# A graph network's edge scores: four-pair waits before the scatters, a full score ring, hot rows turned before the sums, mix steps over pairs 6 to 74

## Chip, cores and metric

One Trainium2 chip, one core. The time is the device time of one execution in microseconds (us): the median of three runs.

## The reference, cut to what matters

Two layers of a graph network over 625 nodes and 20,000 edges, 256 channels. The change lies wholly in layer 0, in the stage that computes one score per edge and head, and beside which the "mix" block of the layer is computed:

```python
# layer 0, graph attention (xn: layernorm of x; 4 heads of 64)
xl = (xn @ W_l).reshape(625, 4, 64); xr = (xn @ W_r).reshape(625, 4, 64)
e = leaky_relu(xl[src] + xr[dst], 0.2)
score = einsum('ehd,hd->eh', e, att)            # one score per edge and head
alpha = softmax of score over the edges of one dst
agg = segment_sum(alpha * xl[src], dst)
# layer 0, mix block on the same xn (8 heads of 32, rank 4)
h = layernorm(xn); xm = h @ Wx + bx
q, k, v = softmax(xm @ Wq), softmax over nodes(xm @ Wk), xm @ Wv
fx = (q @ (k.T @ v)) @ Wo + bo + xn
mix = gelu(layernorm(fx) @ W1 + b1) @ W2 + b2 + fx
x = x + gnn + mix        # then two-expert feed-forward, and layer 1
```

## The kernel before, in words

The edges are first sorted into buckets by (tile of dst, tile of src), 25 buckets, in 184 columns of 125 edges each (`SORTED`). Two columns are a pair, so there are 92 pairs (`PAIRS`). For each column the kernel has two one-hot matrices (the node of dst, the node of src) and works so:

- VectorE, `make_hots` (L1248): builds the one-hots of a pair, two pairs ahead.
- TensorE, `turn_hots` (L621 to L623): turns both one-hots of a column and multiplies them (the counts) into bank 4 or 5. It waits for the one-hots and for `counted`, the earlier `add_counts` on that bank.
- ScalarE, `copy_hots` (L1997): copies the turned hots from the bank to `hot`.
- TensorE, `sum_rows` (L643): eight matmuls a pair, four for each column, that gather and add the rows xl[src] + xr[dst] of 125 edges from the split tables `x_hi` and `x_lo`. The address of the tile comes from registers that `load_rows` loads.
- ScalarE, `read_rows` (L2006, L2007): absolute value of the sums into `weighed` (`tc`), and signals `z_read`.
- VectorE, `weigh` (L1273): times `att`; `add_counts` (L1267): adds a column's counts to `cnt`; `score` (L1281): the sum over a head, to `sc_ring`, signals `scored`.
- GpSimd, `scatter` (L2243): two indirect DMAs a pair, one for each column, into two tables in HBM (`pair_scores`). A scatter into a table waits for the landing of the last one into the same table (`scattered0`, `scattered1`), and the first of a pair waits for `scored`, too.

Each engine runs its instructions in the order in which they are written. The loops over the pairs are

```python
# TensorE                          # VectorE                      # ScalarE
sum_rows(i)                        make_hots(i + 2)               copy_hots(2i + 2)
turn_hots(2i + 2)                  add_counts(2i + 2)             copy_hots(2i + 3)
turn_hots(2i + 3)                  weigh(i)                       read_rows(i)
mix(i)                             add_counts(2i + 3)             mix(i)
load_rows(i + 1)                   score(i); load_counts; mix(i)
```

`mix(i)` is the piece of the mix block whose key in `MIX` is i: a part on TensorE, on ScalarE and on VectorE, in most pairs none. Hidden tiles `m1` take eight pairs in a row, output tiles `m2` five. When all scatters have landed, SyncE loads the two score tables back (`arena<-pair_scores`), and the attention of layer 0 begins; ScalarE takes the logarithm of the counts in between. Apart from these logarithms nothing of the kernel is written beside the end of the scatters.

Of the kernel before, what the change touches and what calls it, by code (L numbers as in the profile page):

```python
# [30 lines left out]
N, D, E = 625, 256, 20000  # L31
P, T = 125, 5
K2 = D // 128
CHUNKS = [(0, 375, (0, 1, 2)), (375, 250, (3, 4))]
H = 4
# [18 lines left out]
PAIRS = SORTED // 2  # L54
# [5 lines left out]
CHOSEN = 3  # L60
MARKS = SORTED + 1
HOTS = 3
SCORED = 16
MIX_BANKS = 3
ROW = D + H
SUM_BANKS = (6, 7, 3)


MIX = {"ln1": 6, "mixh": 8, "turned": 10, "xm": 11, "qkv_in": 12, "softened": 14, "turned_kq": 15, "kv": 17, "qkv": 18,
       "attn": 20, "ln2": 22, "h2": 23, "h2T": 25, "m1": 26, "m2": 35, "added": 40}  # L70


SORTING = {"member": 1, "sums": 3, "block_counts": 4, "begun": 6, "columns": 7, "ident16": 8, "owners_read": 11,
# [58 lines left out]
def after(eng, sem, value):  # L132

    if not (isinstance(value, int) and value <= 0):
        eng.wait_ge(sem, value)
# [35 lines left out]
def build(nc, x_in, src_in, dst_in, base_in, order_in, vec0_in, vec1_in, fb_in, w0_in, w1_in, w2_in, mixw_in, exp0_in,  # L171
          exp0o_in, exp1_in, exp1o_in, exp1r_in, rope_in, out):
    ctx = ExitStack()
    with ctx:
        sems = {}

        def sem(name):
            if name not in sems:
                sems[name] = ctx.enter_context(nc.semaphore(name))
            return sems[name]  # L180

        def sb(name, shape, dt=F32):
            return ctx.enter_context(nc.sbuf_tensor(name, shape, dt))
# [6 lines left out]
        pair_scores = [nc.dram_tensor(f"pair_scores{i}", [N * NC + P, H], F32).ap() for i in range(2)]  # L190
# [62 lines left out]
        at_rows, at_counts = sb("at_rows", [1, SORTED, 2], I32), sb("at_counts", [1, SORTED], I32)  # L253
        spare_cell = sb("spare_cell", [P, 1])
        by_head = sb("by_head", [P, T, 2, H])
        sc_ring = sb("sc_ring", [P, SCORED, 2, H])
        cnt = sb("cnt", [P, T, N])
        mask_words = sb("mask_words", [128, (T * N + 1) // 2])
        nmask = mask_words[0:P, :].bitcast(BF16)[:, 0:T * N].rearrange("p (t n) -> p t n", t=T)
# [8 lines left out]
        hi_rows, lo_rows = (f[0:P, :, :, :].rearrange("p t w d -> p (t w d)") for f in (x_hi, x_lo))  # L268
        at = 2 * T * 2 * ROW + HOTS * 2 * 2 * P
        slot_parts = arena[0:P, at:at + BUCKETS * EC].rearrange("p (b j) -> p b j", b=BUCKETS)  # L270
        w_by_att = arena[:, at:at + K2 * 2 * D].rearrange("p (k n) -> p k n", k=K2)
        at += BUCKETS * EC
        assert at <= ARENA - FF // 128 * (D + N)
        at = ARENA - FF // 128 * N
# [9 lines left out]
        at = 6 * EC  # L284
# [35 lines left out]
        at = ARENA - FF // 128 * (D + N)  # L320
# [10 lines left out]
        at = 5 * H * NC  # L331
# [3 lines left out]
        at = 0  # L335
# [7 lines left out]
        at = 2 * IN1  # L343
# [78 lines left out]
        def read_out(eng, *key):  # L422

            last = {}
            for name, (b, _, n) in ticket.items():
                if name[:len(key)] == key:
                    last[b] = max(last.get(b, 0), n)
            assert last, key
            for b, n in last.items():
                eng.wait_ge(free[b], n)  # L430
# [33 lines left out]
        def _(pe):  # L464
# [18 lines left out]
            def to_fm(name, src):  # L483

                for k in range(K2):
                    for c, (off, w, tiles) in enumerate(CHUNKS):
                        bank, done = group((name, k, c))
                        for t in tiles:
                            mm = pe.transpose(bank[:, t * P - off:t * P - off + P],
                                              src[:, t, k * 128:(k + 1) * 128], ident[0:P, 0:P])  # L490
                        mm.then_inc(done, 1)
# [20 lines left out]
            def linear_fm(name, f, weights, m_tiles, ks=K2):  # L512

                for m in range(m_tiles):
                    for c, (off, w, _) in enumerate(CHUNKS):
                        bank, done = group((name, m, c))
                        for k in range(ks):
                            mm = pe.matmul(bank[:, 0:w], W(weights, k)[:, m * 128:(m + 1) * 128],
                                           f[:, k, off:off + w], start=(k == 0), stop=(k == ks - 1))
                        mm.then_inc(done, 1)  # L520
# [94 lines left out]
            def turn_hots(c):  # L615

                pe.wait_ge(sem("onehot"), c // 2 + 1)
                after(pe, sem("counted"), c - 1)
                bank = banks[4 + c % 2]
                to_d, to_s = (onehot[:, c // 2 % TAKEN, :, c % 2 * 2 + w] for w in range(2))  # L620
                pe.matmul(bank[0:P, 0:P], to_d, ident16[:, :], start=True, stop=True)  # L621
                pe.matmul(bank[0:P, P:2 * P], to_s, ident16[:, :], start=True, stop=True)  # L622
                pe.matmul(bank[0:P, 2 * P:3 * P], to_d, to_s, start=True, stop=True).then_inc(sem("turned_hots"), 1)  # L623
# [3 lines left out]
            def load_rows(i):  # L627

                _, rows_at[i] = nc.values_load_multi_w_load_instructions(
                    at_rows[0:1, 2 * i:2 * i + 2, :].rearrange("p c w -> p (c w)"), engines=[mybir.EngineType.PE],  # L630
                    min_val=0, max_val=(2 * T - 1) * ROW,
                    skip_runtime_bounds_check_because="each is a sum of tile steps over the buckets begun, a tile's offset")

            def sum_rows(i):

                rows = rows_at.pop(i)
                for c in range(2):
                    pe.wait_ge(sem("hot"), 2 * i + c + 1)
                    after(pe, sem("z_read"), 2 * i + c - 2)
                    n = 0  # L640
                    for w in range(2):
                        for part in (hi_rows, lo_rows):
                            mm = pe.matmul(banks[SUM_BANKS[(2 * i + c) % 3]][0:P, 0:ROW], hot[0:P, i % HOTS, c, w, :],  # L643
                                           part[:, bass.ds(rows[2 * c + w], ROW)], start=(n == 0), stop=(n == 3))
                            n += 1
                    mm.then_inc(sem("z_made"), 1)
# [18 lines left out]
            def mix(i):  # L665

                if i == MIX["turned"]:
                    pe.wait_ge(sem("w0_in"), 16)
                    pe.wait_ge(sem("mixh"), 1)
                    to_fm("mixhT", ta)  # L670
                elif i == MIX["xm"]:
                    read_out(pe, "mixhT")
                    linear_fm("xm", fb_, "wx", K2)
                elif i == MIX["qkv_in"]:
                    read_out(pe, "xm")
# [7 lines left out]
                    for c, (off, w, _) in enumerate(CHUNKS):  # L683
# [4 lines left out]
                        mm.then_inc(done, 1)  # L688
                elif i == MIX["turned_kq"]:
                    pe.wait_ge(sem("ksoft"), 1)  # L690
# [5 lines left out]
                    for c, (off, w, tiles) in enumerate(CHUNKS):  # L696
# [3 lines left out]
                        mm.then_inc(done, 1)  # L700
                elif i == MIX["kv"]:
                    read_out(pe, "kN")
# [4 lines left out]
                    mm.then_inc(done, 1)  # L707
                elif i == MIX["qkv"]:
                    read_out(pe, "kv")
# [41 lines left out]
            turn_hots(0)  # L751
            turn_hots(1)
            for i in range(PAIRS):
                sum_rows(i)
                for c in (2 * i + 2, 2 * i + 3):
                    if c < SORTED:
                        turn_hots(c)
                mix(i)
                if i + 1 < PAIRS:
                    load_rows(i + 1)  # L760
# [261 lines left out]
        def _(dve):  # L1022
            own = Chain(dve, sem("dve_own"))
            v = nc.vector
# [39 lines left out]
            def from_fm(name, dst):  # L1064

                for c, (off, w, _) in enumerate(CHUNKS):
                    bank, freed = got(dve, (name, 1, c))
                    v.tensor_copy(dst[:, 1, off:off + w], bank[:, 0:w]).then_inc(freed, 1)
# [185 lines left out]
            def load_counts(i):  # L1254

                _, count_at[i] = nc.values_load_multi_w_load_instructions(
                    at_counts[0:1, 2 * i:2 * i + 2], engines=[mybir.EngineType.DVE], min_val=0, max_val=T * N - P,
                    skip_runtime_bounds_check_because="each is a sum of steps over the buckets begun, a bucket's offset")
# [16 lines left out]

            def score(i):

                for w in range(2):
                    after(dve, sem(f"scattered{w}"), 16 * (i - SCORED + 1))
                own.fence()  # L1280
                v.tensor_reduce(sc_ring[:, i % SCORED, :, :].rearrange("p c h -> p (c h)"),  # L1281
                                weighed[:, i % 2, :, :, :].rearrange("p c h d -> p (c h) d"), AX.X, ALU.add)\
                    .then_inc(sem("scored"), 1)

# [893 lines left out]
        def _(pool):  # L2178
            p = nc.gpsimd
# [57 lines left out]

            def scatter(c):
                which, i = c % 2, c // 2
                if which == 0:  # L2240
                    pool.wait_ge(sem("scored"), i + 1)
                after(pool, sem(f"scattered{which}"), 16 * i)
                p.indirect_dma_start(  # L2243
                    out=pair_scores[which], in_=sc_ring[:, i % SCORED, which, :], in_offset=None,
                    out_offset=bass.IndirectOffsetOnAxis(ap=pair_cells[:, c:c + 1], axis=0))\
                    .then_inc(sem(f"scattered{which}"), 16)

# [8 lines left out]
            for c in range(SORTED):  # L2256
                scatter(c)
# [231 lines left out]
```

## Time and profile before

| | |
|---|---|
| median of three runs | 1112.62 us (1112.42 to 1114.56) |
| the profiled execution | 1119.57 us, span 1117.8 us |
| TensorE matmul, VectorE, ScalarE, GpSimd busy | 862.5, 766.6, 352.7, 375.2 us |
| `scatter`, L2243 | 184 indirect DMAs, 226.6 us busy, 144.5 us idle before them |
| `sum_rows`, L643 from `x_hi` and from `x_lo` | 368 and 368 matmuls, 119.9 and 102.8 us |
| `weigh` L1273, `score` L1281 | 92 and 92, 64.0 and 63.8 us |

Spans are counted from the first instruction, and the execution's own time lies 1.8 us above its span. The busy time of an engine says little by itself here: most engines work in short pieces that wait for each other, and what matters is which piece is last. The granted clock of TensorE (PEclk) is 1.00 at 2.4 GHz and 0.50 at 1.2 GHz.

### The profile page before, as it was taken

The page shows a single profiled execution, that of the slowest core. Times are in us where ns is not written, and L with a number is a line of the kernel's source. Part 1 is how long each engine was busy: PE and PEld are TensorE (multiplying, and loading weights), DVE is VectorE, ACT ScalarE, POOL GpSimd, SP SyncE. Part 2 cuts the span into 40 slices and gives each one's busy share as a digit, 9 for nine tenths or more (in the row PEclk, how much of TensorE's full clock was granted, in tenths as well). Part 3 has the DMA queues.
Part 4 walks back from the last instruction along what each step waited for, and adds up shares of the span by engine and source line. Part 5 has one row for each costly group of instructions (what it writes and reads, how often), then busy time and mean ns, then how long its engine had stood idle before and what let it go on. Part 6 is the DMA issues. An engine that isn't in the chain of part 4 may idle for free.

```text
span 1117.8 us, 18660 instructions
## 1 busy us (share of the span) xinstructions
PE 862.5 (77%) x5483; PEld 736.2 (66%) x5483; DVE 766.6 (69%) x1980; ACT 352.7 (32%) x1096; POOL 375.2 (34%) x321
## 2 busy tenths in 40 slices
PE   4889679699888881017639999895896787699996
PEld 3578567588766660017538999783586476689895
DVE  7778777855777771028977888577788755766635
ACT  0277434273455553015401111101362062112120
POOL 3287646455677666500002222150000000211104
PEclk9988888699899996558858999996898798699999
DMA  8830000000000000089028999970000000688893
GB/s 282 256 119 1 3 2 3 2 3 2 3 3 4 4 2 3 2 195 229 25 65 282 313 321 318 349 231 23 1 1 1 0 2 14 242 300 296 302 328 95
DMA packets 38282, 129.39 MB, mean 116 GB/s; under 512 B 12885, under 2 KB 20929, under 8 KB 29913
## 3 DMA queue, kind: packets, MB, share of 16 engines
q1 hardware_dynamic: 21742, 112.64, 30.8%
q0 software_dynamic: 10464, 8.67, 4.5%
q10 hardware_dynamic: 5992, 7.04, 1.8%
q8 instruction: 43, 0.70, 0.3%
q14 instruction: 41, 0.34, 0.1%
HBM read 108.83 MB, written 19.26 MB: 115 GB/s over the span
## 4 chain that ended last, share of the span: by engine, by line
PE 57%; DVE 18%; DMA 11%; issue 7%; POOL 4%; ACT 2%; DVEq 0%; POOLq 0%; SPq 0%; ACTq 0%
PE bank L854 12%; PE bank L643 9%; PE bank L865 6%; DMA arena<-pair_scores 4%; PE bank L582 4%; PE bank L787 3%; DMA pair_scores<-sc_ring,pair_cells 2%; PE bank L621 2%; PE bank L623 2%; POOL arena L2277 2%; POOL pair_scores L2243 2%; DMA arena<-slot_y,sloti 2%; PE bank L953 2%; PE bank L622 2%; PE bank L653 2%
## 5 line engine op out<-in xcount | busy, mean ns | idle before, releaser
L2243 POOL DMA_INDIRECT pair_scores<-sc_ring,pair_cells x184 | 226.6, 1232 | 144.5 <-issue 70.8
L2267 POOL DMA_INDIRECT arena<-row_tab,ids x42 | 57.5, 1369 | 501.6 <-DVE ids L1660 494.2
L854 PE MATMUL bank<-arena 128*128 128x128 f32 x1480 | 180.6, 280 | 2.6 <-DMA arena<-in_exp 2.6
L854 PEld LDWEIGHTS bank<-arena 128*128 128x128 f32 x1480 | 174.7, 196 | 4.8 <-DMA arena<-in_exp 4.0
L643 PE MATMUL bank<-x_hi,hot 125*125 x368 | 119.9, 346 | 17.4 <-ACT tc L2007 9.9
L1997 ACT ACTIVATE hot<-bank 125x250 fp32r<-125x250 f32 x184 | 68.8, 379 | 163.8 <-PE bank L623 163.5
L776 PE MATMUL bank<-ident,arena 125*125 125x125 f32 x260 | 44.9, 306 | 85.3 <-ACT arena L2054 84.1
L1273 DVE TENSOR_TENSOR tc<-tc,vec 125x512 f32<-125x512 f32 x92 | 64.0, 696 | 56.8 <-ACT tc L2007 56.8
L643 PE MATMUL bank<-x_lo,hot 125*125 x368 | 102.8, 299 | 0.0
L643 PEld LDWEIGHTS bank<-x_hi,hot 125*125 125x125 f32 x368 | 73.1, 199 | 44.4 <-issue 43.7
L865 PE MATMUL bank<-arena 128*128 128x256 f32 (+1 forms) x404 | 99.1, 389 | 2.9 <-issue 2.9
L776 PEld LDWEIGHTS bank<-ident,arena 125*125 125x125 f32 x260 | 40.0, 214 | 90.1 <-issue 77.9
L865 PEld LDWEIGHTS bank<-arena 128*128 128x128 f32 (+1 forms) x404 | 73.1, 192 | 17.0 <-issue 9.2
L2054 ACT ACTIVATE arena<-arena,rneg 125x625 f32<-125x625 f32 (+4 forms) x60 | 44.9, 748 | 115.2 <-DVE rneg L1474 78.0
L643 PEld LDWEIGHTS bank<-x_lo,hot 125*125 125x125 f32 x368 | 74.3, 202 | 0.6
L2125 ACT ACTIVATE arena<-bank 128x512 f32<-128x512 f32 (+2 forms) x76 | 34.4, 453 | 125.1 <-PE bank L854 124.9
L621 PE MATMUL bank<-ident,mask_words 125*125 125x125 bf16 x184 | 48.6, 264 | 27.5 <-DVE cnt L1267 19.7
L1267 DVE TENSOR_TENSOR cnt<-cnt,bank 125x125 f32 x184 | 51.4, 279 | 22.4 <-ACT hot L1997 21.5
L2006 ACT ACTIVATE tc<-bank 125x256 f32<-125x256 f32 x184 | 66.5, 393 | 0.3 <-PE bank L643 0.3
L1281 DVE TENSOR_REDUCE sc_ring<-tc 125x8 f32<-125x520 f32 x92 | 63.8, 694 | 0.4 <-issue 0.3
L2235 POOL TENSOR_SCALAR fmaps<-iota_c,tab 125x185 bf16<-125x185 f16 x40 | 49.2, 1247 | 43.3 <-DVEq L1153 33.9
L1673 DVE TENSOR_TENSOR arena<-bank,arena 128x512 f32<-128x512 f32 (+2 forms) x76 | 37.2, 508 | 37.2 <-ACT arena L2125 37.1
(397 smaller groups left out, 1747.0 us busy)
## 6 DMA issues: line engine op xcount, KB each, us to landing
arena<-in_exp SPq DMA_DIRECT2D x25, 1024.0 KB, 7.1
arena<-in_exp SPq DMA_DIRECT2D x17, 1386.0 KB, 6.3
arena<-in_exp0o SPq DMA_DIRECT2D x25, 512.0 KB, 7.2
pair_scores<-cnt SPq DMA_DIRECT2D x10, 1093.8 KB
arena<-in_exp1o SPq DMA_DIRECT2D x17, 640.0 KB
arena<-pair_scores SPq DMA_DIRECT2D x7, 1093.8 KB
slot_y<-arena ACTq DMA_DIRECT2D x34, 128.0 KB, 6.4
fmaps<-pair_scores SPq DMA_DIRECT2D x3, 1093.8 KB
```

What stands on the lines that cost most here:

```text
L621: pe.matmul(bank[0:P, 0:P], to_d, ident16[:, :], start=True, stop=True)
L643: mm = pe.matmul(banks[SUM_BANKS[(2 * i + c) % 3]][0:P, 0:ROW], hot[0:P, i % HOTS, c, w, :], part[:, bass.ds(rows[2 * c + w], ROW)], start ...
L776: mm = pe.transpose(bank[0:P, t * P - off:t * P - off + P], prob[:, i % 3, t * P:(t + 1) * P], ident[0:P, 0:P])
L854: mm = pe.matmul(banks[1 + 2 * q + buf][0:rows, i * SLOTS:(i + 1) * SLOTS], w_in(s, q, k, m, rows), xsT[:, s, k, :], start=(k == 0), stop= ...
L865: mm = pe.matmul(banks[5 + s][:, 0:D], hid[0:rows, s, m, :], w_out(s, m), start=(m == 0), stop=(m == len(flat) - 1))
L1267: v.tensor_tensor(to, to, banks[4 + c % 2][0:P, 2 * P:3 * P], ALU.add).then_inc(sem("counted"), 1)
L1273: own.note(v.tensor_tensor(rows, rows, Vt(0, "att").rearrange("p (h d) -> p h d", h=H).unsqueeze(1) .to_broadcast([P, 2, H, HD]), ALU.mult))
L1281: v.tensor_reduce(sc_ring[:, i % SCORED, :, :].rearrange("p c h -> p (c h)"), weighed[:, i % 2, :, :, :].rearrange("p c h d -> p (c h) d") ...
L1997: a.activation(hot[0:P, c // 2 % HOTS, c % 2, :, :].rearrange("p w n -> p (w n)"), banks[4 + c % 2][0:P, 0:2 * P], ACT.Copy).then_inc(sem( ...
L2006: a.activation(rows[:, c, :, 0:HD], bank[0:P, 0:D].rearrange("p (h d) -> p h d", h=H), ACT.Abs, scale=0.4)
L2243: p.indirect_dma_start(out=pair_scores[which], in_=sc_ring[:, i % SCORED, which, :], in_offset=None, out_offset=bass.IndirectOffsetOnAxis( ...
L2267: p.indirect_dma_start(out=xs[:, q, :], out_offset=None, in_=tab, in_offset=bass.IndirectOffsetOnAxis(ap=ids[:, q, :], axis=0))\
```

## The change

Four edits. The scatters of the first four pairs wait for `scored` pair by pair as before; from pair 4 on only every fourth pair waits, and then for all four pairs. `sc_ring` has 92 places in place of 16, lies in a part of `arena` that the sorting has left, and `score` waits for no scatter. On TensorE `turn_hots` of the next pair stands ahead of `sum_rows` of this one. The steps of the mix block lie farther apart, and end at pair 74 in place of 40.

```diff
-SCORED = 16
+SCORED = PAIRS
+AHEAD = 4
-MIX = {"ln1": 6, "mixh": 8, "turned": 10, "xm": 11, "qkv_in": 12, "softened": 14, "turned_kq": 15, "kv": 17, "qkv": 18,
-       "attn": 20, "ln2": 22, "h2": 23, "h2T": 25, "m1": 26, "m2": 35, "added": 40}
+MIX = {"ln1": 6, "mixh": 9, "turned": 12, "xm": 15, "qkv_in": 18, "softened": 21, "turned_kq": 24, "kv": 27, "qkv": 30,
+       "attn": 33, "ln2": 37, "h2": 41, "h2T": 45, "m1": 50, "m2": 66, "added": 74}
...
-        sc_ring = sb("sc_ring", [P, SCORED, 2, H])
+        sc_ring = arena[0:P, at + K2 * 2 * D:at + K2 * 2 * D + SCORED * 2 * H].rearrange("p (s c h) -> p s c h", s=SCORED, c=2)
...
             for i in range(PAIRS):
-                sum_rows(i)
                 for c in (2 * i + 2, 2 * i + 3):
                     if c < SORTED:
                         turn_hots(c)
+                sum_rows(i)
                 mix(i)
...
             def score(i):
-                for w in range(2):
-                    after(dve, sem(f"scattered{w}"), 16 * (i - SCORED + 1))
                 own.fence()
-                v.tensor_reduce(sc_ring[:, i % SCORED, :, :].rearrange("p c h -> p (c h)"),
+                v.tensor_reduce(sc_ring[:, i, :, :].rearrange("p c h -> p (c h)"),
...
             def scatter(c):
                 which, i = c % 2, c // 2
-                if which == 0:
-                    pool.wait_ge(sem("scored"), i + 1)
+                if which == 0 and (i < AHEAD or i % AHEAD == 0):
+                    pool.wait_ge(sem("scored"), i + 1 if i < AHEAD else min(i + AHEAD, PAIRS))
                 after(pool, sem(f"scattered{which}"), 16 * i)
                 p.indirect_dma_start(
-                    out=pair_scores[which], in_=sc_ring[:, i % SCORED, which, :], in_offset=None,
+                    out=pair_scores[which], in_=sc_ring[:, i, which, :], in_offset=None,
```

## Rows read from the trace of the kernel before

**Rows 1.** The chain that ended last, in time: start us, length us, what.
```profile
281.61 2.61 DMA pair_scores<-sc_ring,pair_cells
...
452.05 3.19 DMA pair_scores<-sc_ring,pair_cells
...
474.72 4.05 DMA pair_scores<-sc_ring,pair_cells
480.05 12.99 DMA arena<-pair_scores
```

**Rows 2.** `score`: durations in ns, first and last start; busy | idle before it.
```profile
L1281 DVE TENSOR_REDUCE sc_ring<-tc x92: 681/695/696, 111.8 to 424.2; 125x8 f32<-125x520 f32 x92
...
L1281 DVE TENSOR_REDUCE sc_ring<-tc 125x8 f32<-125x520 f32 x92 | 63.8, 694 | 0.4 <-issue 0.3
```

**Rows 3.** GpSimd in order of time: start, length, and the idle time before.
```profile
310.53 1.19 POOL L2243 DMA_INDIRECT pair_scores<-sc_ring,pair_cells  x1 [0.78 <-issue]
312.03 1.19 POOL L2243 DMA_INDIRECT pair_scores<-sc_ring,pair_cells  x1 [0.30 <-issue]
313.92 1.19 POOL L2243 DMA_INDIRECT pair_scores<-sc_ring,pair_cells  x1 [0.70 <-DVE sc_ring L1281]
```

**Rows 4.** One undisturbed pair, all engines in order of time, clock 1.00.
```profile
326.36 0.28 DVE L1267 TENSOR_TENSOR cnt<-cnt,bank 125x125 f32 x1
...
326.78 0.30 PE L621 MATMUL bank<-ident,mask_words 125*125 125x125 bf16 x1
...
327.03 0.32 PE L623 MATMUL bank<-mask_words 125*125 125x125 bf16 x1
...
327.39 0.38 ACT L1997 ACTIVATE hot<-bank 125x250 fp32r<-125x250 f32 x1 [0.31 <-PE bank L623]
327.39 0.38 PE L643 MATMUL bank<-x_hi,hot 125*125 x1
...
327.98 0.41 ACT L2006 ACTIVATE tc<-bank 125x256 f32<-125x256 f32 x1
328.24 0.21 ACT L2007 ACTIVATE tc<-bank 125x4 f32<-125x4 f32 x1
...
328.35 0.38 PE L643 MATMUL bank<-x_hi,hot 125*125 x1 [0.21 <-ACT tc L2007]
...
328.49 0.69 DVE L1273 TENSOR_TENSOR tc<-tc,vec 125x512 f32<-125x512 f32 x1 [0.69 <-ACT tc L2007]
...
328.81 0.28 PE L643 MATMUL bank<-x_lo,hot 125*125 x1
...
328.93 0.22 PE L621 MATMUL bank<-ident,mask_words 125*125 125x125 bf16 x1
...
329.10 0.28 DVE L1267 TENSOR_TENSOR cnt<-cnt,bank 125x125 f32 x1
```

**Rows 5.** Busy us (and instructions) of each engine by stretch, PEclk, DMA.
```profile
305.60:422.00 116.40, 101.05 (x593) 79.03 (x593) 86.86 (x212) 61.86 (x258) 79.71 (x65) 1.00 0.08 3
128.10:131.50 3.40, 2.38 (x14) 1.65 (x13) 3.30 (x15) 1.45 (x6) 2.37 (x3) 1.00 0.07 2
...
285.10:288.50 3.40, 2.51 (x14) 1.87 (x14) 3.37 (x7) 1.38 (x6) 2.98 (x2) 1.00 0.04 1
288.50:295.30 6.80, 6.36 (x32) 5.92 (x32) 4.77 (x12) 3.68 (x16) 4.81 (x5) 0.50 0.08 3
537.70:554.70 17.00, 10.90 (x94) 10.30 (x93) 16.13 (x45) 7.58 (x21) 0.00 (x0) 1.00 0.01 2
223.70:251.00 27.30, 27.30 (x159) 22.77 (x158) 15.41 (x36) 19.37 (x62) 15.71 (x14) 1.00 0.07 3
```

**Rows 6.** One `sum_rows` at clock 0.50, from the order of time.
```profile
291.65 0.58 PE L643 MATMUL bank<-x_hi,hot 125*125 x1 [0.20 <-ACT hot L1997]
...
292.68 0.42 PE L643 MATMUL bank<-x_hi,hot 125*125 x1
...
293.32 0.42 PE L643 MATMUL bank<-x_lo,hot 125*125 x1
```

## The prediction

> **What bounds the kernel now.** I read the chain of waits first, then the lines of `score` and `scatter`, then one pair instruction by instruction, then the clock by stretch.
>
> The chain shows where the stage ends. The last scatter is issued at 474.72 and lands 4.05 us later, at 478.77; the tables are loaded back from 480.05 on, and nothing else is on the chain there [rows 1]. `score` runs 92 times, the first starting at 111.8 and the last at 424.2 [rows 2]. So in the last 54 us the scores are all there and only scatters are left: GpSimd and its DMA queue bound the end of the stage, not the scoring. What is to be seen of the scatters: the first of a pair starts 3.39 us after the first of the pair before (310.53 to 313.92), while the second follows the first by 1.50, 1.19 of work and 0.30 between [rows 3]. The other 1.89 is no work. A scatter lands 2.61 us after its start [rows 1], and the first of a pair has two waits, for the score and for that landing; it starts 0.78 us after the engine's last work, though the score is long there. 3.39 is 2.61 and 0.78.
>
> Ahead of that, the scoring has its own pace: 326.36 to 329.10, 2.74 us a pair [rows 4]. The scoring took 424.2 - 111.8 = 312.4 us for 91 steps from score to score. 27 pairs carry a mix step; the 64 others at 2.74 make 175.4, so the 27 take 137.0.
>
> **The scatters.** From pair 4 on, three pairs in four have one wait in their first scatter, as every second scatter has today. Such a pair costs two times 1.49, that is 2.98, or the landing and 0.30 if that is more (2.91 at 2.61). The fourth keeps 3.39. The mean is 3.08, and with the late landings that the end shows (3.19 to 4.05 [rows 1]) some 3.3. The price is at the end: the last four pairs start only after the last score. With 0.30 for the release, three pairs at 3.5 and 0.30 (3.5 lies between the 3.19 and 4.05 of the end), one gap of 1.49 and the last landing of 4.05, the tail from the last score is 17.2 us. In exchange for the 54 us of now, that is a gain of 36.7 if the last score stays at 424.9.
>
> **The ring.** `score` sits behind no scatter in the trace: VectorE is idle before it for 0.4 us in all 92 [rows 2]. The write is the same size elsewhere in SBUF. That edit is worth nothing; its cover is that VectorE waits for ScalarE 0.69 us a pair before `weigh` [rows 4].
>
> **Hot rows turned first.** This is what moves the pace of the scoring. The loop that gives 2.74 now goes: `add_counts` of the odd column ends at 326.64, which lets TensorE turn the next odd column at 326.78 (0.14); its last matmul ends at 327.35, and ScalarE copies from 327.39 (0.61 after 326.78); it then reads both sums, which TensorE made before it turned, until 328.45; `weigh` starts at 328.49, the odd `add_counts` 0.61 later at 329.10, and takes 0.28 [rows 4]. The sums lie beside this, in the shade.
>
> In the new order the sums of a pair stand behind the turning of the same odd column, and ScalarE's reading waits for them. The engines' queues are in order, so the loop is now: odd turn, both sums, reading of the second sum, `weigh`, odd `add_counts`, odd turn. Its length at clock 1.00:
> - odd turn to first sum: at least 0.37 (0.25 to its last matmul and 0.12 to the next), at most 0.61, as now with the register load between (327.39 - 326.78); I take 0.43, near the lower end, since `load_rows` is no longer there.
> - first to second sum: 0.58, as from 328.35 to the group that follows at 328.93.
> - second sum, first matmul to end: 328.35 to 329.09, 0.74.
> - to ScalarE 0.04, reading 327.98 to 328.45, 0.47.
> - to `weigh` 0.04, to `add_counts` 0.61, its length 0.28, to the turn 0.14.
>
> Sum 3.33 [all rows 4], against 2.74: 0.59 us more for each pair in which this loop decides. With the ends of the first term it is 3.27 to 3.51. The even column's turn and `load_rows` fit into the 1.5 us that TensorE waits.
>
> **The mix steps.** They are the same instructions, spread. A step that TensorE or VectorE fills keeps its length: in the run of `m1` TensorE is busy 27.30 of 27.30 us, 3.77 us a pair [rows 5], above 3.33. Small ones are taken in by the longer wait; I estimate 4 us of the 137.0. Spreading alone gives the scoring nothing, since each step delayed its own pair and not its neighbour. It would give the scatters an even supply, but a scatter pair at 3.3 is then no longer slower than the scoring.
>
> So at full clock: 64 x 3.33 = 213.1, and 133.0: 346, the last score at 112.5 + 346 = 458.5. The four pairs before may still hold up the last four by 1 to 2 us. With the tail of 17.2 the last landing is at 477, against 478.8. **The two large effects cancel**: 34 us later scores, 36.7 us shorter tail.
>
> **The clock.** Now the row that decides. At 2.74 us TensorE is busy 101.05 of 116.40 us, 593 matmuls, 5.1 a microsecond, and the clock is 1.00 throughout [rows 5]. At 3.33 the same 14 matmuls are 4.2 a microsecond, busy 0.87 x 2.74 / 3.33 = 0.71. Stretches of just that kind are in the trace: 128.1 to 131.5 (14 matmuls in 3.4 us, busy 2.38) and 285.1 to 288.5 (14, busy 2.51). After each of them the clock was 0.50, and after the second one it came back only after 6.8 us in which TensorE was busy for 6.36 and issued 4.7 a microsecond [rows 5]. Against it stands 537.7 to 554.7, held at 1.00 with 10.90 busy of 17.00 [rows 5], though of denser float32 matmuls.
>
> At the lower clock the loop grows by its TensorE parts: first to second sum 1.03 (291.65 to 292.68), second sum to end 1.06 (292.68 to 293.74) [rows 6], against 0.58 and 0.74. That is +0.77, a pair of 4.10 us, 3.4 matmuls a microsecond: sparser than the stretch from which it took 6.8 us to come back. In the old order the sums lie in the shade, so a low clock costs a pair next to nothing; in the new one it is paid in full, and the loop's own slack keeps it low. I expect the low clock for most undisturbed pairs, with 1.00 again during and a few microseconds behind the heavy mix steps: 44 of 64 pairs, 34 us. The mix steps that begin at the low clock (some seven of them with 2 to 4 us of TensorE work, and the first of `m1` and of `m2`) take longer too; I estimate 20 us, with 5 and 35 as ends.
>
> Sum: last score 458.5 + 34 + 20 = 512.5; tail 17.2; last landing 529.7 against 478.8: +51 us. The profiled execution of 1119.6 becomes 1170.5; the median of the runs lies 7 us below the profiled one, so 1112.6 + 51 = 1163.
>
> The Trainium skill, "TensorE: Matmul & The Clock Gate", Part 1 (The HAM clock gate), puts the fall of the clock down to an idle window, and the release to sustained activity. The new loop is never idle for more than about 1 us, so read strictly that rule keeps the clock up and gives the rival "clock stays", 1112. The stretch from 285.1 speaks against the strict reading: TensorE was never quiet for long there, and the clock fell.
>
> **The rivals.**
> 1. The clock stays at 1.00, and gain and loss cancel. For it: 537.7 to 554.7 [rows 5]. Against it: both stretches of 14 matmuls. The time: 477 - 478.8, about -1.5, 1111; with the ends of the first term (64 x -0.06 to 64 x +0.18) 1107 to 1123. The point from which it decides: 4.2 matmuls a microsecond suffice.
> 2. The clock falls now and then and recovers. Half the loss: 1120 to 1140, 1130.
> 3. The other side, faster: the loop of the scoring doesn't lengthen, because TensorE's odd turn is not what is waited for. Then the last score is at 112.5 + 175.4 + 133 = 421, the tail 17.2, but the scatters at 3.3 to 3.4 a pair from 113.5 on end near 440: -39, 1074. It decides if `weigh` and the odd `add_counts` of a pair end before the next odd turn would start anyway, which the order of VectorE's queue speaks against. Between this and 1 lies a loop of some 3.0: -20, 1092.
> 4. The waits of four pairs starve GpSimd all along. A batch needs 12.3 us and some 0.8 for late landings, four scores need 13.3 or more; it is always ready in time. That costs only the tail, which is in every case above.
>
> **How the numbers follow.** Forecast (low clock for most pairs, 1140 to 1178) 0.68; rival 2 0.11; rival 1 0.12, of which 0.05 slower, 0.05 within, 0.02 faster by over 0.2% (2.2 us, about what a measurement of this kernel can tell from no change); rival 3 with its middle 0.09. Faster 0.11 and a little for a chain that I misread, 0.14; same 0.06; slower 0.80. The range takes in the forecast with both ends of the 20 us, rival 2, and the upper part of rival 1: 1113 to 1177.
>
> **What would show it.** In the line of `score`: starts 3.3 apart at clock 1.00 and 4.1 at 0.50, the last near 511. In the clock row: 0.5 in most slices from 113 to 500. TensorE's odd turn waits for `add_counts`, and ScalarE's L2006 for L643, which it hardly does now. On GpSimd 1.49 between most scatters of a batch, and waits for `score` between batches; the last scatter lands 15 to 18 us after the last score. It is wrong if the undisturbed pairs stay at 2.74 (the loop), or if the clock row stays at 9 and 10 (the clock), and wrong in size if the heavy mix steps bring the clock back for longer.

## The result, and the profile after

The changed kernel takes 1157.75 us (median of 4 runs, 1152.28 to 1159.30), the kernel before 1113.06 beside it (1112.42 to 1114.56): a ratio of 1.0387, 95% interval [1.0356, 1.0419]. It is slower by 44.7 us. The profiled execution took 1158.33 us, with a span of 1156.6 and a mean granted clock of 0.803, where before it was 0.878.

The page of the changed kernel, the granted clock in 40 slices and then the groups of the scoring (busy, mean ns of one | idle before it, and what ended most of it):

```profile
PEclk9978558567579685555865999997989699699999
...
L2242 POOL DMA_INDIRECT pair_scores<-arena,pair_cells x184 | 227.6, 1237 | 184.8 <-DVE arena L1280 107.0
...
L1274 DVE TENSOR_TENSOR tc<-tc,vec 125x512 f32<-125x512 f32 x92 | 63.7, 692 | 137.7 <-ACT tc L2006 137.7
L644 PE MATMUL bank<-x_hi,hot 125*125 x368 | 143.3, 400 | 0.0
L622 PE MATMUL bank<-ident,mask_words 125*125 125x125 bf16 x184 | 56.3, 306 | 101.2 <-DVE cnt L1268 97.2
...
L2005 ACT ACTIVATE tc<-bank 125x256 f32<-125x256 f32 x184 | 70.6, 384 | 65.1 <-PE bank L644 64.8
```

Three engines wait in a ring: TensorE's turn (L622) for VectorE's `add_counts`, ScalarE's reading (L2005) for TensorE's sums, VectorE's `weigh` (L1274) for ScalarE's reading. GpSimd's scatter (L2242) now waits mostly for `score`, which was long done in the last 54 us before [rows 2].

The line of `score` (ns, then first and last start), and the end of the chain that ended last, in order of time:

```profile
L1280 DVE TENSOR_REDUCE arena<-tc x92: 682/689/695, 113.2 to 499.9; 125x8 f32<-125x520 f32 x92
```

```profile
497.64 5.04 DMA pair_scores<-arena,pair_cells
...
503.54 1.19 POOL pair_scores L2242
...
505.04 2.99 DMA pair_scores<-arena,pair_cells
...
508.31 3.72 DMA pair_scores<-arena,pair_cells
...
512.32 3.65 DMA pair_scores<-arena,pair_cells
...
516.26 3.51 DMA pair_scores<-arena,pair_cells
...
521.05 13.31 DMA arena<-pair_scores
```

The last score starts at 499.9, where it was 424.2 [rows 2]; the last scatter lands at 516.26 + 3.51 = 519.77, where it was 478.77 [rows 1]. So the stage ends 41.0 us later. What follows takes 636.8 us, before 639.0. The two spans are 38.8 us apart, the two medians 44.7, since the profiled execution of before was 6.5 us above its median.

**The loop at each clock.** The changed kernel in order of time, first at clock 1.00 (TensorE has a piece of the mix block behind these sums, from 176.37 on; the steps walked here lie ahead of it or on other engines):

```profile
174.96 0.30 PE L622 MATMUL bank<-ident,mask_words 125*125 125x125 bf16 x1 [0.86 <-DVE cnt L1268]
...
175.30 0.36 PE L644 MATMUL bank<-x_hi,hot 125*125 x1
...
175.86 0.29 PE L644 MATMUL bank<-x_hi,hot 125*125 x1
...
176.54 0.38 ACT L2005 ACTIVATE tc<-bank 125x256 f32<-125x256 f32 x1
...
177.03 0.69 DVE L1274 TENSOR_TENSOR tc<-tc,vec 125x512 f32<-125x512 f32 x1 [1.09 <-ACT tc L2006]
177.63 0.28 DVE L1268 TENSOR_TENSOR cnt<-cnt,bank 125x125 f32 x1
```

and then at clock 0.50:

```profile
444.23 0.42 PE L644 MATMUL bank<-x_hi,hot 125*125 x1
...
445.34 0.38 ACT L2005 ACTIVATE tc<-bank 125x256 f32<-125x256 f32 x1 [0.35 <-PE bank L644]
...
445.82 0.69 DVE L1274 TENSOR_TENSOR tc<-tc,vec 125x512 f32<-125x512 f32 x1 [1.96 <-ACT tc L2006]
446.43 0.28 DVE L1268 TENSOR_TENSOR cnt<-cnt,bank 125x125 f32 x1
...
446.85 0.34 PE L622 MATMUL bank<-ident,mask_words 125*125 125x125 bf16 x1 [1.24 <-DVE cnt L1268]
...
447.20 0.56 PE L644 MATMUL bank<-x_hi,hot 125*125 x1
...
448.20 0.42 PE L644 MATMUL bank<-x_hi,hot 125*125 x1
```

The loop can be walked in both: odd turn, first sum, second sum, its reading, `weigh`, odd `add_counts`, odd turn. At 1.00 the steps are 0.34, 0.56, 0.68, 0.49, 0.60 and, for the length of `add_counts` with the release, 0.42, taken from the pair below: 3.1 us. At 0.50 they are 0.35, 1.00, 1.11, 0.48, 0.61, 0.42: 3.97 us. Only the two steps through the sums have grown, by 0.44 and 0.43. TensorE's `sum_rows` has moved from the shade into the loop, and with it the clock.

The clock itself, busy us and instructions of each engine by stretch, as in [rows 5]:

```profile
111.50:166.00 54.50, 33.54 (x170) 31.10 (x170) 34.17 (x90) 18.90 (x73) 21.35 (x17) 0.50 0.04 2
169.50:176.40 6.90, 4.68 (x36) 4.17 (x34) 4.06 (x11) 3.44 (x14) 5.65 (x5) 1.00 0.08 2
183.20:186.60 3.40, 2.16 (x14) 1.84 (x14) 2.26 (x6) 1.52 (x7) 2.79 (x3) 1.00 0.04 1
...
398.00:422.00 24.00, 24.00 (x144) 21.90 (x143) 11.15 (x27) 7.32 (x27) 9.53 (x8) 1.00 0.05 2
425.50:500.00 74.50, 51.53 (x260) 48.15 (x260) 39.82 (x95) 30.32 (x115) 48.70 (x40) 0.50 0.07 3
```

The run of `m2` has the clock at 1.00 with 6.0 matmuls a microsecond and TensorE never idle. Behind it the undisturbed pairs run for 74.5 us at 0.50: 3.5 matmuls a microsecond, busy 51.53 of 74.50. The stretch ahead of the fall at 186.6 has 14 matmuls in 3.4 us, like the two stretches of before that preceded a fall [rows 5]. Between the first and the last score the clock is low for 260.4 of 386.7 us; before it was 47.8 of 312.4.

### The profile page after: what moved, and what is told of

Its sections match the earlier page's. It is cut to its first block, busy times and chain, and to the rows that moved or that the text cites. A ratio compares the mean times of both kernels' runs of the same rounds, so it can differ in the third digit from the quotient of the medians.

```text
span 1156.6 us, 18518 instructions
## 1 busy us (share of the span) xinstructions
PE 884.0 (76%) x5483; PEld 776.7 (67%) x5483; DVE 763.1 (66%) x1980; ACT 365.7 (32%) x1096; POOL 376.2 (33%) x321
## 4 chain that ended last, share of the span: by engine, by line
PE 58%; DVE 18%; DMA 10%; issue 8%; POOL 2%; ACT 2%; DVEq 1%; POOLq 0%; SPq 0%; ACTq 0%
PE bank L855 12%; PE bank L644 11%; PE bank L866 6%; DMA arena<-pair_scores 4%; PE bank L583 4%; PE bank L788 3%; PE bank L622 2%; DMA pair_scores<-arena,pair_cells 2%; POOL arena L2276 2%; DVE cnt L1268 2%; DMA arena<-slot_y,sloti 2%; PE bank L662 2%; PE bank L654 2%; PE bank L954 2%; PE bank L777 1%
## 5 line engine op out<-in xcount | busy, mean ns | idle before, releaser
L2242 POOL DMA_INDIRECT pair_scores<-arena,pair_cells x184 | 227.6, 1237 | 184.8 <-DVE arena L1280 107.0
L1274 DVE TENSOR_TENSOR tc<-tc,vec 125x512 f32<-125x512 f32 x92 | 63.7, 692 | 137.7 <-ACT tc L2006 137.7
L644 PE MATMUL bank<-x_hi,hot 125*125 x368 | 143.3, 400 | 0.0
L622 PE MATMUL bank<-ident,mask_words 125*125 125x125 bf16 x184 | 56.3, 306 | 101.2 <-DVE cnt L1268 97.2
L644 PE MATMUL bank<-x_lo,hot 125*125 x368 | 132.0, 369 | 0.0
L622 PEld LDWEIGHTS bank<-ident,mask_words 125*125 125x125 bf16 x184 | 37.2, 202 | 118.2 <-issue 97.2
L644 PEld LDWEIGHTS bank<-x_lo,hot 125*125 125x125 f32 x368 | 102.0, 277 | 0.0
L644 PEld LDWEIGHTS bank<-x_hi,hot 125*125 125x125 f32 x368 | 101.2, 275 | 0.1
L2005 ACT ACTIVATE tc<-bank 125x256 f32<-125x256 f32 x184 | 70.6, 384 | 65.1 <-PE bank L644 64.8
L1280 DVE TENSOR_REDUCE arena<-tc 125x8 f32<-125x520 f32 x92 | 63.3, 688 | 0.0
```

The costliest lines, as they stand in the source:

```text
L1274: own.note(v.tensor_tensor(rows, rows, Vt(0, "att").rearrange("p (h d) -> p h d", h=H).unsqueeze(1) .to_broadcast([P, 2, H, HD]), ALU.mult))
L1280: v.tensor_reduce(sc_ring[:, i, :, :].rearrange("p c h -> p (c h)"), weighed[:, i % 2, :, :, :].rearrange("p c h d -> p (c h) d"), AX.X, A ...
L2005: a.activation(rows[:, c, :, 0:HD], bank[0:P, 0:D].rearrange("p (h d) -> p h d", h=H), ACT.Abs, scale=0.4)
L2242: p.indirect_dma_start(out=pair_scores[which], in_=sc_ring[:, i, which, :], in_offset=None, out_offset=bass.IndirectOffsetOnAxis(ap=pair_c ...
```

## The experiments

Ten kernels. The numbers that compare them come from each one's trace: the starts of `score`, the 64 steps from score to score without a mix step (their sum and median), the time at the low clock between the first and the last score, and the last landing. Each ratio is to the kernel before on the same chip, whose medians were 1110.7 to 1113.5 us. Where two medians that were not taken side by side are compared, such as those of the changed kernel and of an experiment, some 3 us of the difference can come from that. The last landing of the kernel before, 478.77, comes from an execution 6.5 us above its median, so landings compared with it can look several us too early.

| kernel | median us | ratio, 95% interval | last score starts | 64 steps, sum (median) | low clock us | last landing |
|---|---|---|---|---|---|---|
| before | 1113.06 | | 424.2 | 174.9 (2.74) | 47.8 | 478.77 |
| changed | 1157.75 | 1.0387 [1.0356, 1.0419] | 499.9 | 240.9 (3.97) | 260.4 | 519.77 |
| order alone | 1145.98 | 1.0315 [1.0275, 1.0354] | 498.3 | 249.0 (3.97) | 274.4 | 507.39 |
| changed, order undone | 1095.94 | 0.9877 [0.9842, 0.9913] | 423.8 | 175.1 (2.74) | 51.2 | 456.81 |
| spread alone | 1091.38 | 0.9835 [0.9801, 0.9870] | 424.4 | 175.8 (2.74) | 55.0 | 451.85 |
| waits and ring alone | 1110.71 | 0.9992 [0.9969, 1.0014] | 423.1 | 174.6 (2.74) | 47.8 | 473.41 |
| changed, filler | 1119.54 | 1.0074 [1.0046, 1.0102] | 458.3 | 206.2 (3.13) | 45.6 | 484.60 |
| changed, counts first | 1085.13 | 0.9789 [0.9753, 0.9825] | 405.7 | 157.1 (2.36) | 41.0 | 446.85 |
| before, waits swapped | 1097.06 | 0.9875 [0.9849, 0.9901] | 423.4 | 174.7 (2.74) | 47.8 | 463.44 |
| before, spread and swapped | 1080.96 | 0.9745 [0.9714, 0.9776] | 424.6 | 176.1 (2.74) | 61.5 | 444.63 |
| the same, turned and counted first | 1077.95 | 0.9675 [0.9633, 0.9717] | 413.5 | 162.4 (2.44) | 58.0 | 442.65 |
| the same, counted first only | 1072.47 | 0.9630 [0.9581, 0.9679] | 405.6 | 157.1 (2.44) | 37.5 | 435.87 |

**1. The new order alone.** In the kernel before, `sum_rows(i)` behind the turning; nothing else.

```diff
-                sum_rows(i)
                 for c in (2 * i + 2, 2 * i + 3):
                     if c < SORTED:
                         turn_hots(c)
+                sum_rows(i)
```

> The kernel before with one edit: hot rows turned ahead of the sums. Theory (the new order puts the sums into the loop that sets the pace of the scoring, and that slower loop keeps the clock low): score to score about 3.1 us at clock 1.00 and 3.97 at 0.50, low clock from pair 45 to the end, last score near 500, last landing some 6 us behind it; median 1135 to 1145, so nearly the whole loss and more than the changed kernel's gain at the scatters can pay back. Rival (the loss comes from the spread mix steps or from the waits of four pairs, the order is harmless): 1110 to 1116, 2.74 us a pair.

Measured: 1145.98 us, 35 above the 1110.7 of before on its chip and 1 above the range that I gave. `score` and the stretch 305.6 to 422.0, whose clock was 1.00 with 593 matmuls [rows 5]:

```profile
L1281 DVE TENSOR_REDUCE sc_ring<-tc x92: 684/695/697, 112.8 to 498.3; 125x8 f32<-125x520 f32 x92
```

```profile
305.60:422.00 116.40, 79.82 (x410) 75.29 (x410) 61.13 (x149) 45.06 (x174) 70.85 (x59) 0.50 0.07 3
```

One moved line reproduces the long steps, the low clock and the late scores. The same stretch holds 410 matmuls, 3.5 a microsecond, at 0.50. Here the scatters follow close behind the scores, though each pair still waits by itself: the last lands 9 us after the last score starts, and 8.4 after it ends at 499.01.

```profile
504.73 2.66 DMA pair_scores<-sc_ring,pair_cells
```

That is why the order costs 35 us here and some 60 in 2. The last score comes 74 us later than before, but 54 us of scatters stood behind it there, and slow scores leave hardly any backlog: the last landing is 28.6 us later.

**2. The changed kernel with the order undone.** The same edit backwards.

> The changed kernel with one edit undone: sums ahead of the turning again. Theory: 2.74 us a pair, clock 1.00 in undisturbed pairs, last score at 420 to 426; scatters at about 3.1 to 3.3 us a pair end near 440; median 1070 to 1082, clearly faster than before. Rival (waits of four pairs or the spread do the harm): 1113 or slower.

Measured: 1095.94, 62 us under the changed kernel, and 15 under the 1110.7 of before on its chip. The steps are 2.74 again and the last score starts at 423.8:

```profile
L1280 DVE TENSOR_REDUCE arena<-tc x92: 679/686/694, 111.9 to 423.8; 125x8 f32<-125x520 f32 x92
```

So the order is the whole of the loss, and without it the other three parts together are worth 15 us; the median is 14 us above the range that I gave. The chain of waits ends with a landing at 453.60 + 3.21 = 456.81, 33 us after the last score starts. The scatters, not the scores, bound the end again: over the 40 pairs from 45 on they start 3.50 us apart, where I expected 3.1 to 3.3.

**3. The mix steps spread, alone.** The new table of mix steps in the kernel before.

> The kernel before with the mix steps spread alone. Theory: the scoring takes as long as before (last score 420 to 426), but GpSimd, at its 3.4 to 3.7 us a pair, is no longer starved during the mix steps, so the scatters end near 450: median 1083 to 1095. Rival, as I wrote in the prediction (spreading alone gives nothing): 1110 to 1115.

Measured: 1091.38, with the last landing at 451.85, 27 us earlier, while the last score stays at 424.4. The scoring gained nothing, as predicted. The scatters did: they no longer starve during a dense run of mix steps, and reach the end with less behind them. This edit alone is at least as good as the three parts together (2). The medians are 19.3 us apart; the rest of the 27 may lie in the traced execution of before, which was 6.5 us above its median.

**4. The waits of four pairs and the ring of 92, alone.** In the kernel before, with the edits of `sc_ring` and `score` as in the change, not shown here:

```diff
-                if which == 0:
-                    pool.wait_ge(sem("scored"), i + 1)
+                if which == 0 and (i < AHEAD or i % AHEAD == 0):
+                    pool.wait_ge(sem("scored"), i + 1 if i < AHEAD else min(i + AHEAD, PAIRS))
```

> The kernel before with the waits of four pairs and the ring of 92 alone. Theory: scatters at 3.1 to 3.3 us a pair once scores are in stock, but starved up to pair 40 as before; 51 pairs from 285 on end near 455: median 1085 to 1097. Rival (the landing of the last scatter and not the wait for the score sets 3.4 us, so nothing is gained): 1110 to 1115.

Measured: 1110.71, ratio 0.9992: no change that can be told. My range is missed by 14 us and the rival's time came out, but not for the rival's reason, as GpSimd shows in order of time:

```profile
279.39 1.18 POOL L2242 DMA_INDIRECT pair_scores<-arena,pair_cells  x1 [8.75 <-DVE arena L1280]
280.88 1.19 POOL L2242 DMA_INDIRECT pair_scores<-arena,pair_cells  x1 [0.30 <-issue]
...
310.53 1.19 POOL L2242 DMA_INDIRECT pair_scores<-arena,pair_cells  x1 [0.30 <-issue]
312.02 1.19 POOL L2242 DMA_INDIRECT pair_scores<-arena,pair_cells  x1 [0.30 <-issue]
313.51 1.19 POOL L2242 DMA_INDIRECT pair_scores<-arena,pair_cells  x1 [0.30 <-issue]
```

Inside a batch the scatters are 1.49 apart where a pair took 3.39 [rows 3], as computed. But at 279.39 GpSimd has waited 8.75 us for the fourth score of a batch, in a stretch where the mix steps make scores scarce. Pair 4 waited longer still, 10.66 us. Pair 40's first scatter starts at 294.36, where it started at 285.21 before. Over the 40 pairs from 45 on the pace is 3.39 us against 3.63; the gain repays the delay. The last landing is 5.4 us earlier than in the traced execution of before, which was 6.5 us above its median; the medians are the same.

**5. The changed kernel with filler.** Six (`FILL`) more bf16 matmuls of 125 columns a pair, at the point where TensorE is about to wait; their results go to columns that nothing reads.

```diff
                 sum_rows(i)
+                after(pe, sem("z_read"), 2 * i)
+                for _ in range(FILL):
+                    pe.matmul(banks[SUM_BANKS[(2 * i + 2) % 3]][0:P, 300:300 + P], ident16[:, :], ident16[:, :],
+                              start=True, stop=True, skip_group_check=True)
```

> The changed kernel with six extra bf16 matmuls of 125 columns a pair on TensorE behind the sums, into unread columns of a free bank; their results go nowhere. They lie in the time in which TensorE waits. Theory (the low clock is paid in the new loop, 3.97 against 3.1 us a pair): clock 1.00 in undisturbed pairs, 3.1 to 3.2 us a pair; 49 pairs at 3.97 give back some 40 us; last score near 458, median 1112 to 1122. Rival (the clock reading goes with the slower loop but does not cause it, or added work lengthens it): 3.97 or more a pair, median 1157 or slower.

Measured: 1119.54, 38 us under the changed kernel, for 552 matmuls more. Windows of it, then `score`:

```profile
425.00:458.00 33.00, 24.48 (x211) 22.92 (x211) 21.50 (x53) 17.62 (x65) 23.18 (x19) 1.00 0.08 3
```

```profile
L1285 DVE TENSOR_REDUCE arena<-tc x92: 680/686/695, 112.8 to 458.3; 125x8 f32<-125x520 f32 x92
```

In this stretch TensorE has 6.4 matmuls a microsecond and the clock is 1.00. The median step is 3.13, close to the 3.1 of the loop at full clock; 8 of the 64 steps are still 3.97. The clock is a cause of its own, not a sign of the waiting: the loop's order is the same, only TensorE's pauses are filled, and 38 us are gone. The filler isn't free where TensorE has no pause: the pairs with `m1` take 4.16 us in place of 3.75. The 24 us that are left above the kernel of 2 are the longer loop and this cost.

**6. The changed kernel with the odd `add_counts` ahead of `weigh`.** This takes VectorE's `weigh` out of the loop and leaves the new order on TensorE.

```diff
                     add_counts(2 * i + 2)
-                weigh(i)
                 if i + 1 < PAIRS:
                     add_counts(2 * i + 3)
+                weigh(i)
                 score(i)
```

> The changed kernel with VectorE's add_counts of the odd column ahead of weigh. Theory (the loop runs sum, reading, weigh, odd add_counts, odd turn): the turn no longer waits for the sums of its own pair, the loop is cut; 2.4 to 2.8 us a pair, clock 1.00, last score near 410 to 425, then the scatters bound the end as in the kernel with the order undone: median 1088 to 1100. Rival (TensorE's order as such costs the time): 3.1 us a pair or more, median above 1130.

Measured: 1085.13, 73 us under the changed kernel and 3 below the range that I gave. In order of time:

```profile
384.08 0.28 DVE L1268 TENSOR_TENSOR cnt<-cnt,bank 125x125 f32 x1 [0.20 <-DVE cnt L1268]
...
384.29 0.68 DVE L1274 TENSOR_TENSOR tc<-tc,vec 125x512 f32<-125x512 f32 x1
...
384.52 0.30 PE L622 MATMUL bank<-ident,mask_words 125*125 125x125 bf16 x1
```

The odd turn starts at 384.52, 0.23 after `weigh` starts and before it ends. The steps are 2.36, shorter than in the kernel before, and the low clock falls to 41.0 us. The new order on TensorE costs some 60 us only because VectorE's queue closes the loop; one swap there opens it.

**7. The kernel before with the two waits of a scatter swapped.** The wait for the scatter's own landing is written first, the wait for `score` second.

```diff
                 which, i = c % 2, c // 2
+                after(pool, sem(f"scattered{which}"), 16 * i)
                 if which == 0:
                     pool.wait_ge(sem("scored"), i + 1)
-                after(pool, sem(f"scattered{which}"), 16 * i)
```

> The kernel before with one edit at the scatters: the wait for the last landing is written ahead of the wait for the score, so that the scatter instruction itself carries the landing and the score is waited for separately and ahead. Theory (with two waits the start comes 0.86 us after the landing, with one 0.30): 2.98 us a pair with a timely landing, mean 3.3 to 3.4 after pair 45 in place of 3.63, and no delay of a batch: last landing near 463, median 1092 to 1102. Rival: the order in which the waits are written is nothing to the engine, 1108 to 1113.

Measured: 1097.06, 13.6 us under the kernel before, for two exchanged lines. GpSimd in order of time, at the place of [rows 3]:

```profile
311.96 1.19 POOL L2243 DMA_INDIRECT pair_scores<-sc_ring,pair_cells  x1 [0.31 <-issue]
313.45 1.18 POOL L2243 DMA_INDIRECT pair_scores<-sc_ring,pair_cells  x1 [0.30 <-issue]
314.94 1.19 POOL L2243 DMA_INDIRECT pair_scores<-sc_ring,pair_cells  x1 [0.30 <-issue]
...
322.18 1.68 POOL L2243 DMA_INDIRECT pair_scores<-sc_ring,pair_cells  x1 [1.06 <-DMA pair_scores<-sc_ring,pair_cells]
```

The 0.78 ahead of a pair's first scatter is gone. The chains show where it was. First the kernel before, then this one:

```profile
455.25 0.02 issue
455.27 0.02 POOLq L135
455.29 0.82 issue
456.11 3.50 DMA pair_scores<-sc_ring,pair_cells
```

```profile
449.51 0.29 issue
449.80 3.58 DMA pair_scores<-sc_ring,pair_cells
```

The wait written first is carried by the scatter itself. The one written second becomes an instruction of its own ahead of it (POOLq; L135 is the helper `after`), and in the kernel before that one waited for the landing, which came last.

This is what the waits of four pairs were to bring (4), for every pair, and without making any scatter wait for a score that it doesn't use.

**8. The kernel before, spread and swapped.** The edits of 3 and 7 together.

> The kernel before with spread mix steps and the swapped waits, ring of 16, old order on TensorE. Theory: both gains add, scatters at 3.3 us a pair nearly from the start, last landing 430 to 442, median 1070 to 1083. Rival (late landings take back what the shorter start gives): 1088 to 1092 as with the spread alone.

Measured: 1080.96. The two gains nearly add: 0.9835 x 0.9875 is 0.9712, and 0.9745 [0.9714, 0.9776] was found. A likely reason, not tested: they take from the same backlog of scatters, which after the spreading is smaller.

**9. The same with both orders of TensorE and VectorE changed.** Turned first, and the odd `add_counts` first.

> Spread mix steps, swapped waits, hot rows turned first, and add_counts of the odd column ahead of weigh; ring of 16. Theory: scoring at 2.36 us an undisturbed pair, so the scatters are hardly ever without a score and run at 3.4 us a pair from 113.5 on: last landing 425 to 438, median 1062 to 1076, below the 1081 of spread and swapped alone. Rival (the scatters are bound by their own landings already in that kernel): 1077 to 1083.

Measured: 1077.95, two us above the range that I gave. The scores end 11 us earlier and the last landing is only 2 us earlier: with the first scatter of a pair starting 3.44 us apart, the scatters bound the end, and the time lies in the rival's range.

**10. The same, with TensorE in its old order.** Only the VectorE swap on top of 8.

> As the kernel with all four edits, but with TensorE's old order, sums ahead of the turning. Theory: the odd add_counts behind weigh was the closing link of the loop in either order, so the order no longer matters: 2.4 to 2.5 us an undisturbed pair and a median within 5 us of that kernel. Rival (only the new order profits): 2.74 us a pair, 1078 to 1083.

Measured: 1072.47, the fastest kernel here, 3.7% under the kernel before and 7.4% under the changed one. The rival that only the new order of TensorE profits from the swap has fallen: the old one profits too, 2.74 to 2.44 us a step. The order on TensorE matters little beside it, though the medians are 5.5 us apart where I expected 5 at most. That this kernel is better than 9 rests on intervals that overlap, [0.9581, 0.9679] and [0.9633, 0.9717].

## Why the prediction was right

The forecast was 1163 and slower; 1157.75 was measured. The mechanism of the loss, the loop through the sums and the low clock in it, is the one that the runs show. The gain that was set against it came out in size, but not by the cause that was named, and that is luck. By its own steps:

- **The loop.** Moving the turning ahead closes a loop through both sums: shown by 1 and 2 (+35 alone, -62 undone). Predicted 3.33 us at clock 1.00, measured 3.10. Most of the difference is in two terms: the first, for which I took 0.43 with a lower end of 0.37, is 0.34; and from the second sum to its reading it is 0.68, not 0.74 and 0.04. In the filler kernel (5) the loop has its full clock in all but 8 of its 64 steps, and they take 206.2 us, where the sum had 213.1.
- **The low clock.** Predicted 4.10 us for 44 of 64 pairs; measured 3.97 for 49, with 14 at 3.10 to 3.44 and the last at 1.66. The 64 steps sum to 240.9, where the prediction had 213.1 + 34 = 247. The filler (5) shows the clock to be causal: -38 us.
- **The mix steps.** Predicted 133 + 20 = 153 us for the 27, measured 145.8. The 20 was too large: the 27 grew by 8.8 over the 137.0, not by 16. With the line above, 6 us and 7 us less, and a first score 1.4 us later than before, this is the whole difference between the last score's end of 512.5 in the sum and the 500.6 measured.
- **The tail.** Predicted 17.2 us from the last score, measured 519.77 - 500.6 = 19.1. The last batch of four didn't start when the last score was there: a scatter begun at 497.64 took 5.04 us to land, and pair 88 started only at 503.54. The four landings of the chain after it took 2.99 to 3.72, about what the sum had for them (3.5, and 4.05 for the last). The last landing is at 519.8, where the sum had 529.7.
- **The ring.** No run took it alone. With the waits (4) it moved nothing that can be told.

Four statements of it were wrong:

- The shorter tail was put down to the waits of four pairs. Run 1 has none of them, and its tail is 8.4 us: scores that come 3.97 us apart are slow enough for the scatters, at 3.4 to 3.6 us a pair, to follow them. In the changed kernel the tail fell from 53.9 to 19.1 us, 34.8 where the sum had 36.7. Beside the slow scores the three other edits cost time. The changed kernel's ratio is 1.0387 [1.0356, 1.0419], that of the order alone 1.0315 [1.0275, 1.0354], some 8 us with intervals that just don't overlap, and its last scatter lands 12.4 us later with a last score only 1.6 later. The other 10.7 are the longer tail, in which the last batch waits for four scores; no run parts the three edits there.

- "Spreading alone gives the scoring nothing" is right, and what I made of it is not: I gave the even supply of the scatters no price, and it is worth some 19 us by itself (3). In the kernel before, the scatters run behind the scores because they first starved, then couldn't catch up at 3.4 to 3.6 us a pair against 2.74. I had only read their end.
- "It is always ready in time", of the batches of four, was worked out with the steps of a changed kernel whose scores are spread. With the table of before (4) the batches wait for scores, up to 10.66 us. With the spread table (2 against 3) they cost too, if anything: 1095.94 against 1091.38. In 2 pair 4 starts at 137.62 us, in 3 at 126.71, and of those 11 us 5 are left at the last landing. So with the scoring at its old pace the gain isn't 36.7 us: undoing the order, it was 15 us in all, and 3 says that the spreading brought it.
- "3.39 is 2.61 and 0.78": the 0.78 is idle time after GpSimd's last work, not the time from the landing to the start. That time is 0.86, and this landing took 2.53. The sum is the same, so the error cost nothing.

Taken together, the three other edits gain 15 us where the scatters are behind (2) and lose some 8 where the scores are slow. What an edit is worth depends on which of the two queues is behind.

The Trainium skill, "TensorE: Matmul & The Clock Gate", Part 1 (The HAM clock gate), ties the fall to an idle window in its table; further down, the same Part tells of a kernel in which short pauses between groups of matmuls came often enough for the clock to go back and forth. Here the clock stood at 0.50 for 74.5 us in which TensorE was busy for 51.53; around the odd turn at 446.85, where the loop waits longest, it was idle for 1.24 us. The trace is nearer to the second than to the table, though here the clock stayed low instead of going back and forth. The measurement decides, and the rival that leant on the idle window (1111 us) didn't come about.

What stays open: why the last seven pairs of scatters land later than the others (medians of 3.1 to 3.7 us, against 2.6 over a kernel) in all kernels but order alone; why 9 is not faster than 10; and which of the three other edits costs the 8 us on top of the order.

## What to carry to other kernels

When two instructions change places in one engine's queue, walk the loop across all queues with the new order, and look for the one in-order neighbour that closes it: here two lines of VectorE's queue decided whether the same TensorE order gave 1158 or 1085 us. If the new loop leaves TensorE waiting, price every TensorE term in it at the low clock too. A queue that bounds the end of a stage may do so because it starved in the middle, so read its starts along the whole stage, and before batching a wait, count what the batch waits for where supply is scarcest. Price a gain at the end of a queue with the pace that the other edits leave it: a backlog shrinks by itself when what feeds it slows down.

## What the runs showed of the hardware

- **Idle-time work made the kernel faster.** 552 matmuls whose results nothing reads took 38 us off (5). Between the first and the last score the clock was low for 45.6 us in place of 260.4.
- **The order of two waits costs 0.56 us a scatter.** A GpSimd scatter starts 0.86 us after the landing that it waits for when the wait for `score` is written first (455.25 to 456.11 in the kernel before), and 0.30 when the landing's wait is written first (449.51 to 449.80 in 7). What is swapped isn't free: in 7 a scatter that waited for `score` started 0.86 us after its end (137.20 to 138.06), where that takes 0.30 in the kernel before.
- **Landings have a tail.** The median is 2.58 to 2.60 us in all kernels, but single ones take over 5: 5.04 in the changed kernel (497.64), 5.2 in 8 (421.28 to 426.5). One late landing holds GpSimd's whole queue: after the one at 497.64 the next scatter but one started 2.58 us after the engine's last work.
